# Sum six units of probabilities per half on GpSimd, and multiply by the inverse denominators on VectorE

## The reference

```python
xn = _layernorm(x)
x = x + _L0_attn_ref(xn, W_qkv, W_o) + _L0_ffn_ref(xn, w_fc, w_proj)

# _L0_attn_ref, H = 16 heads of D_H = 32
qkv = jnp.einsum('bld,ed->ble', x, W_qkv).reshape(b, 3, H, L, D_H)
Q, K, V = (qkv[:, 0], qkv[:, 1], qkv[:, 2])
scores = jnp.einsum('bhqd,bhkd->bhqk', Q, K) * D_H ** (-0.5)
attn = jax.nn.softmax(scores, axis=-1)
out = jnp.einsum('bhqk,bhkd->bhqd', attn, V)
out = out.transpose(0, 2, 1, 3).reshape(b, L, D_IN)
return jnp.einsum('bld,ed->ble', out, W_o)
```

## Time and profile before

| | |
|---|---|
| median of 3 runs | 3328.11 us (3327.81 to 3333.6) |
| the profiled execution, its own time | 3329.19 us |
| its span, first to last instruction | 3327.4 us |
| mean granted TensorE clock | 0.981 |
| busy over the span: TensorE, VectorE, ScalarE, GpSimd | 97%, 74%, 60%, 55% |
| the chain that ended last: TensorE's share | 49% |

### The profile page before, as it was taken

The page is one execution under the profiler, slowest core; times in us unless marked ns, Lnnn a source line. Parts: engine busy times, 40 slices in busy tenths (PEclk is TensorE's granted clock), DMA queues, the critical chain, the costliest instruction groups (busy, mean ns, idle before and its releaser), DMA issues.

```text
span 3327.4 us, 73253 instructions
## 1 busy us (share of the span) xinstructions
PE 3225.1 (97%) x30336; PEld 1541.1 (46%) x30336; DVE 2450.7 (74%) x3456; ACT 1982.9 (60%) x2955; POOL 1831.4 (55%) x658
## 2 busy tenths in 40 slices
PE   3899999999999999998999999999999999999899
PEld 2344444444444444443444444444444444444344
DVE  7666666666676666666888888888888888888644
ACT  4444444444444444441688888888888888888711
POOL 0322323222333332220689889888988988988800
PEclk7899999999999999997899999999999999999999
DMA  4122222223132322224334443433433343343296
GB/s 159 75 87 78 92 91 80 88 83 81 79 81 102 83 85 85 90 68 99 60 77 82 81 81 70 89 76 75 84 80 83 70 89 74 72 87 64 72 336 233
DMA packets 376062, 309.34 MB, mean 93 GB/s; under 512 B 300672, under 2 KB 317056, under 8 KB 365440
## 3 DMA queue, kind: packets, MB, share of 16 engines
q1 hardware_dynamic: 375744, 304.69, 34.4%
HBM read 96.99 MB, written 139.46 MB: 71 GB/s over the span
## 4 chain that ended last, share of the span: by engine, by line
PE 49%; issue 1%; DVE 1%; POOL 1%; ACT 1%; DMA 1%; SPq 0%; POOLq 0%; ACTq 0%; DVEq 0%
PE es_for_maxima_and_scores L1088 26%; PE outputs L1109 13%; PE misc L1143 6%; PE es_for_maxima_and_scores L1184 3%; DVE half_maxima L1019 1%; POOL probs_sum L935 1%; ACT probs L967 0%; DMA k_stackT<-attention_scratch 0%; PE misc L1126 0%; DMA q_stackT<-stack_scratch 0%; POOL out_normed L942 0%; DVE q_stackT L1042 0%; ACT k_stackT L978 0%; ACT k_stackT L973 0%; DMA q_stackT<-maxima_rows 0%
## 5 line engine op out<-in xcount | busy, mean ns | idle before, releaser
L1019 DVE TENSOR_REDUCE half_maxima<-es_for_maxima_and_scores 128x1 f32<-128x512 f32 x2048 | 1275.5, 682 | 249.1 <-PE es_for_maxima_and_scores L1088 233.7
L967 ACT ACTIVATE probs<-es_for_maxima_and_scores,scalars 128x512 f32<-128x512 f32 x2048 | 1247.9, 696 | 316.5 <-PE es_for_maxima_and_scores L1088 313.1
L935 POOL TENSOR_TENSOR probs_sum<-probs_sum,probs 128x2048 f32<-128x2048 f32 x224 | 1026.5, 4583 | 23.2
L1088 PE MATMUL es_for_maxima_and_scores<-k_stackT,q_stackT 96*32 96x512 f16 x8192 | 851.4, 389 | 12.1 <-DMA q_stackT<-stack_scratch 11.2
L1088 PE MATMUL es_for_maxima_and_scores<-q_stackT,k_stackT 98*32 98x512 f16 x8192 | 839.5, 383 | 10.5 <-issue 7.2
L1109 PE MATMUL outputs<-probs,v_rows 128*32 128x512 f32 x4096 | 538.9, 594 | 2.3 <-ACT probs L967 0.8
L403 POOL TENSOR_TENSOR gelu_sum<-gelu_sum,gelu_out 128x1024 f32<-128x1024 f32 x96 | 254.9, 2655 | 451.5 <-ACT gelu_out L578 451.5
L1088 PEld LDWEIGHTS es_for_maxima_and_scores<-q_stackT,k_stackT 98*32 98x32 f16 x8192 | 326.6, 137 | 350.7 <-ACT probs L967 112.4
L935 POOL TENSOR_TENSOR probs_sum<-probs 128x2048 f32<-128x2048 f32 x64 | 293.2, 4581 | 226.3 <-ACT probs L967 226.3
L1088 PEld LDWEIGHTS es_for_maxima_and_scores<-k_stackT,q_stackT 96*32 96x32 f16 x8192 | 244.9, 96 | 314.3 <-DVE half_maxima L1019 172.7
L641 PE MATMUL psA<-x_hi,ternary_fcT 128*128 128x512 f16 x1024 | 388.1, 379 | 1.9 <-DVE x_lo L449 1.4
(11 more groups left out here) (135 smaller groups left out, 3300.6 us busy)
## 6 DMA issues: line engine op xcount, KB each, us to landing
stack_scratch<-hi_hi_lo_hi_rows SPq DMA_DIRECT2D x32, 1536.0 KB, 5.1
stack_scratch<-hi_hi_lo_hi_rows SPq DMA_DIRECT2D x32, 576.0 KB, 5.9
v_scratch<-v_rows_out SPq DMA_DIRECT2D x32, 576.0 KB, 6.9
x_rows<-in_L_attn_x SPq DMA_DIRECT2D x16, 1024.0 KB, 4.9
x_plus_ffn_scratch<-x_rows SPq DMA_DIRECT2D x16, 1024.0 KB, 3.9
v_rows<-v_scratch SPq DMA_DIRECT2D x32, 512.0 KB, 4.5
inverse_denominators<-denominators_scratch SPq DMA_DIRECT2D x256, 64.0 KB, 2.0
attention_scratch<-out_normed SPq DMA_DIRECT2D x64, 256.0 KB, 2.1
```

What stands on the lines that cost most here:

```text
L935: nc.gpsimd.tensor_tensor(acc[:, hf], pr[:, 0] if j == 1 else acc[:, hf], pr[:, j], ALU.add).then_inc(added, 1)
L967: nc.scalar.activation(pr[:, w % 8, h, :], psS[:, bank(g, HG * w + h), :], ACT.Exp, scale=keep["scal"]["escale"]).then_inc(exp_done, 1)
L1019: nc.vector.tensor_reduce(mx[:, slot(n, 2), h, t, kh:kh + 1], psX[:, bank(n, r), :], axis=AX.X, op=ALU.max).then_inc(max_done, 1)
L1088: last = nc.tensor.matmul(out[q:q + 32, :], stationary[:, q:q + 32], moving, start=start, stop=stop)
```

## The change

`POOLED` goes from (6, 5) to (6, 6): in the second half GpSimd makes five adds instead of four, and TensorE's denominators three steps instead of four. The step that stood in unit 1 is gone, and units 2, 3 and 4 hold the three that are left. The multiplication by the inverse denominators leaves GpSimd's program and enters VectorE's, behind the second maximum of its unit; it stands in units 3 and 11 instead of 2 and 9, and the stores of its results in units 4 and 12 instead of 3 and 10.

```diff
-POOLED = (6, 5)
+POOLED = (6, 6)
...
-NORMALISE = {2: (1, 0), 9: (1, 1)}
-STORE = {3: (1, 0), 10: (1, 1)}
-DEN = {1: (1, 1, 0), 2: (1, 1, 1), 3: (1, 1, 2), 4: (1, 1, 3), 10: (0, 0, 0), 11: (0, 0, 1), 12: (0, 0, 2)}
+NORMALISE = {3: (1, 0), 11: (1, 1)}
+STORE = {4: (1, 0), 12: (1, 1)}
+DEN = {2: (1, 1, 0), 3: (1, 1, 1), 4: (1, 1, 2), 10: (0, 0, 0), 11: (0, 0, 1), 12: (0, 0, 2)}
...
                 for w in units:
                     if exists(g) and 1 <= w % 8 < POOLED[w // 8]:
                         add(g, w // 8, w % 8)
-                    if due(NORMALISE, g, w):
-                        normalise(*due(NORMALISE, g, w))
...
+            def normalise(g, hf):
+                dve.wait_ge(inv_loaded, lin(g, 128, 64 * hf + 64))
+                dve.wait_ge(oraw_out, lin(g, 2, hf + 1))
+                wait(dve, ot_stored[hf], lin(g, 16))
+                nc.vector.tensor_tensor(on[:, hf, :], oraw[:, hf, :], rden[:, hf, :], ALU.mult).then_inc(on_ready, 1)
...
                         if k == 0 and due(INVERT, g, w):
                             invert(*due(INVERT, g, w))
+                        if k == 1 and due(NORMALISE, g, w):
+                            normalise(*due(NORMALISE, g, w))
```

## The result

The changed kernel takes 3641.03 us (median of 4, 3634.75 to 3643.88), the kernel before 3329.49 (median of 4, 3327.81 to 3333.6). The ratio is 1.0931 with an interval from 1.0912 to 1.095: about 310 us slower. The profiled execution took 3643.88 us.

What follows compares the result with a forecast made beforehand. TensorE was taken to set the pace, GpSimd next. Terms -19 - 1.5 + 213 + 1 + 22 + 8 = +223 on the span of 3327.4 gave 3551, as median 3552 us; range 3430 to 3620.

Steps and rivals of the forecast that it cites:

- The step less: Unit 1 of each group: one denominator step less on TensorE saves 0.64 us net, -19 us over bodies 1 to 30.
- The add at nothing: GpSimd, second half: one add more costs nothing while TensorE covers it, with 1.1 us a group of room left.
- The phase: Units 3 and 11: VectorE's multiplication comes 0.10 us behind add 2's start and waits for the whole add.
- The lock: GpSimd's add 2 holds VectorE's multiplication at the shared ports; TensorE stalls 3.8 us, 56 times, +213 us.
- Groups 1 and 2: GpSimd enters group 1 late by 1.6 us, so VectorE gets in ahead of add 2 and pays little: +1 us.
- The clock: TensorE's granted clock falls behind stalls; a quarter of the full cost was taken, +22 us, bounds 0 to +90.
- The last group and the steps behind it: Group 30's multiplications queue among VectorE's subtractions, +8 us; the step less behind the last group, -1.5 us.
- hidden and faster: Rival: VectorE gets in ahead of add 2 in both halves, the multiplication fits idle time; 3312 us, chance 0.11.

Runs made afterwards that it cites:

- one maximum earlier: The changed kernel with the multiplication behind the first maximum of units 3 and 11 instead of the second: 3306.02 us, ratio 0.9935.
- the wider memset: The changed kernel with a GpSimd memset of 128 x 512 zeros between add 1 and add 2 of each half: 3307.2 us, ratio 0.9934.

## Why the prediction was right on the cause and short on the time

I predicted 3552 with a range of 3430 to 3620. The kernel took 3641, slower as forecast, but 21 us beyond the range. By its own steps:

- **The step less.** Predicted: group 47.94 us without stalls, and -19 over the groups. Measured: 47.96 where the lock does not catch, and 19 us between the two kernels that differ only in adds and steps. Right. Its -1.5 behind the last group was not measured by itself.
- **The add at nothing.** Right while the multiplications are off GpSimd (578 of 600 us busy and no loss). With them it is the bound, 3339.54.
- **The phase.** Predicted: VectorE 0.10 behind add 2, in both halves. Measured: 0.12, and all caught from group 3 on. This was the step that I held likeliest to fail, and it held.
- **The lock.** Predicted: the multiplication ends 0.56 after the add, TensorE 3.8 us late, 56 times. Measured: 3.70 us in the stall read, 56 times, 207 in place of 213. With a copy in place of the product the wait is gone. The Trainium skill (SBUF — State Buffer, section "SBUF: two separate sides") has the lock as one that the earlier instruction keeps to its end. The runs agree on the lock, with 4.97 us for a product that began 0.12 behind an add. On who is the earlier, and the earlier trace rows differ from it by a little: VectorE's record began 0.05 ahead of GpSimd's, and VectorE waited. What the runs show besides is that a waiting VectorE goes in before GpSimd's next add.
- **Groups 1 and 2.** Predicted +1, with 0.8 at the first and under 0.2 later. The first took 1.83 us, which is 0.85 above the 0.98 of idle time, the second 1.11 and the last 0.69. Right.
- **The clock.** This is the step that failed: "I take a quarter, +22", with 90 as the upper bound. Measured: behind every stall of the stretch read, 2.4 us each. 56 x 2.4 = 134, which is +112 against the forecast and 44 above the bound. Two things were wrong. The likelihood was put low because the pause in the earlier trace rows was nearly twice as long, though nothing in the trace spoke of pauses between 0.23 and 6.5 us. And the bound took its 1.6 us from the one low stretch of the earlier trace rows. That stretch had 3.4 us of work in it, 1.7 us lost, and ten of the twenty behind the stalls are like it. The other ten have 6.0 us of work in them and lost 3.0 each.
- **The last group and the steps behind it.** Predicted +8 and -1.5. From the last transposed maxima to the end it is 227.2 us (3414.9 to 3642.1), before 228.6 (3098.8 to 3327.4): -1.4. The work was late as forecast, and it did cost. The rows below are group 30's second multiplication, TensorE's pause for output tile 2 behind it, and the clock behind the pause:

```profile
3466.56 3.72 DVE L1042 TENSOR_TENSOR out_normed<-out_raw,inverse_denominators 128x512 f32<-128x512 f32 x1
...
3487.51 0.61 PE L1190 MATMUL es_for_maxima_and_scores<-woT_hi,k_stackT 128*128 128x512 f16 x1 [5.22 <-DVE q_stackT L1046]
...
3487.60:3491.60 4.00, 4.00 (x10) 0.50 0.32 101
```

All waits for such tiles are 6.6 us in place of the 1.5 of the earlier trace rows, 5.1 more, and some 4.1 us of work behind the longest ran at the lower level, 2.0 lost: 7.1 us, near the +8. What gave it back is the pause of the earlier trace rows. In the kernel before it is this row:

```profile
3109.15 1.50 PE L1088 MATMUL es_for_maxima_and_scores<-q_stackT,k_stackT 98*32 98x512 f16 x12 [6.58 <-issue]
```

In the changed kernel TensorE has no such pause there, which with the 1.7 us of clock is 8.3 us less. Such a pause stands in the traces of the two kernels that multiply on GpSimd in every group (6.58 us, and 7.74 with the adds only) and in none of the eleven others. The profile names nothing that ended it, so why it is gone is open. The prediction used the pause for the clock and left it itself out of the sum. That the two nearly cancel is luck.

The terms as measured, -19 + 56 x (3.70 + 2.4) - 1.4 + 1 = +322 (the -1.4 is the whole end of the kernel, both terms in it), stand against a span that grew by 314.7. The 7 us between them are 0.13 us a stall. The group says the same: 59.98 us (the multiplication at 2322.41 comes again seven groups later at 2742.27, 59.98 each), less 47.96, leaves 12.02 for two stalls, of which 7.4 are waiting and 4.6 the clock, 2.3 a stall. With 2.3 the sum is +317. The miss of about 90 us is thus +112 of the clock, less 6 of the lock, less 8 of the last group, less these 7.

Of the rivals, hidden and faster was only some tenths of a microsecond of phase away: the kernels of one maximum earlier and of the wider memset are it, 3306 and 3307 against the 3312 given, or 3306 without the pause of 0.22. The reading of the Trainium skill that stood beside it (GPSIMD Engine Reference, section "4.1 Engine selection") is not refuted on speed, 0.68 us against 1.27. But moving the multiplication by itself gave 0.9992 at one place and 1.1129 at another.

## What to carry to other kernels

Before an operation with two SBUF inputs, or one like that of the earlier trace rows, goes to VectorE, look at what GpSimd runs at that moment: what it can cost is the rest of GpSimd's instruction, and the place to ask is late in one, not just behind the start of the next. Such a phase can lock: the stall gives GpSimd the slack that brings it back to the same place each half. When TensorE gets new pauses of some microseconds, price the clock as "after every one" at the upper end, take the length of the slow stretch from more than one row, and keep that in the range.

## What the hardware did that I had not expected

- The granted clock fell after every pause of 3.5 us that was read (20 in a row), after every second of 2.3 us, and after 9 of 23 of 1.4 us. Over 2000 to 2600, work at the lower level lost 47.4 us behind 20 pauses of 3.5, 18.5 us behind 22 of 2.3 (51.2 us idle), and 15.4 us behind 23 of 1.4 (36.5 us idle in all, these and a few others). What decides at the shorter ones, and why the slow stretches behind the long ones are 3.5 us in half of the cases and 6.75 in the other half, is open.
- A memset on GpSimd, which only writes, does not hold VectorE: the multiplication took 0.68 us, beginning 0.06 behind a memset of 0.52.
- VectorE waiting at the lock goes in between two of GpSimd's adds (0.90 us, the first 0.35 of them before the add ends). In the rows read the second add needs the first one's sum and follows 0.15 us behind its end. Whether VectorE would also get in ahead of an instruction that follows at once is not shown. The four adds behind it took 19.00 us together, against 18.71 with nothing at the lock.
